# Third feed-forward: the output projection of an attention tile, moved into the next tile's first group

## The reference, cut to what matters

```python
h = shift_token(x)
q, k, v = split(h @ wqkv, 3)                     # 8 heads of 64
q, k = l2norm(q) * qs, l2norm(k) * ksc           # then rotary
sim = (8 q) k^T      # a window of 64 rows sees itself and the 64 before it
attn = softmax(where(mask, -max, sim))
o = attn @ v
x = x + o @ wo                                   # the projection this change moves
h = layernorm(shift_token(x))
a, g = split(h @ w1 + b1, 2)
x = x + (a * gelu(g)) @ w2 + b2
```

## Time and profile before

| what | us |
|---|---|
| median of three runs | 5603.85 |
| lowest and highest of them | 5593.51, 5620.94 |
| the profiled execution's own time | 5583.52 |
| its span, first to last instruction | 5582.2 |
| mean granted TensorE clock over the span, as a share of full | 0.771 |
| TensorE busy, share of the span | 71% |
| VectorE busy | 54% |
| ScalarE busy | 34% |

### The profile page before, as it was taken

How to read it: one execution, slowest core, us unless ns; L and a number is a source line. 1 busy time by engine, 2 the same in 40 slices (tenths; PEclk the granted TensorE clock), 3 DMA queues, 4 the chain that set the end, 5 groups by cost and what they waited for, 6 DMA issues and landing times.

```text
span 5582.2 us, 94810 instructions
## 1 busy us (share of the span) xinstructions
PE 3985.0 (71%) x39676; PEld 3069.5 (55%) x39676; DVE 3004.8 (54%) x8021; ACT 1910.5 (34%) x4228; POOL 819.3 (15%) x600
## 2 busy tenths in 40 slices
PE   5786958467788787863576858667777777776398
PEld 4574847345555555553455647555544555455377
DVE  4455364335555555556266565656666666665333
ACT  2233232123333333320243242325444455552122
POOL 0000000231111111022500000001121111110544
PEclk6555555688999999985766666668888998897699
DMA  9200000240000000001300000000000000000255
GB/s 262 62 2 1 2 1 2 89 133 1 1 1 1 1 1 1 1 22 24 64 1 1 2 1 2 1 2 1 1 1 1 1 1 1 1 1 17 82 163 139
DMA packets 140860, 152.33 MB, mean 27 GB/s; under 512 B 7808, under 2 KB 128002, under 8 KB 139792
## 3 DMA queue, kind: packets, MB, share of 16 engines
q1 hardware_dynamic: 119024, 128.21, 7.9%
q0 software_dynamic: 21408, 18.05, 1.9%
HBM read 87.38 MB, written 59.76 MB: 26 GB/s over the span
## 4 chain that ended last, share of the span: by engine, by line
PE 48%; DVE 31%; ACT 12%; issue 3%; POOL 3%; DMA 2%; SPq 0%; DVEq 0%; POOLq 0%; ACTq 0%
ACT work L3251 4%; PE banks_lane L801 4%; PE banks_lane L422 3%; PE banks_lane L3688 3%; PE banks_lane L1885 2%; DVE work L2038 2%; PE banks_lane L809 2%; PE banks_lane L3137 2%; PE banks_lane L935 2%; PE banks_lane L3172 2%; PE banks_lane L3117 1%; PE banks_lane L3159 1%; POOL room_l_ffn L569 1%; DVE work L2806 1%; DVE weights L3261 1%
## 5 line engine op out<-in xcount | busy, mean ns | idle before, releaser
L422 PE MATMUL banks_lane<-constants,work 128*128 128x128 f32 x968 | 194.5, 346 | 453.0 <-DVE work L408 206.2
L422 PEld LDWEIGHTS banks_lane<-constants,work 128*128 128x128 f32 x968 | 146.3, 178 | 520.1 <-DVE work L408 193.2
L422 PE MATMUL banks_lane<-constants,weights 128*128 128x128 f32 x596 | 125.0, 346 | 350.0 <-DVE weights L408 94.0
L402 POOL TENSOR_TENSOR weights<-weights,constants 128x4 f32<-128x4 f32 x76 | 78.5, 1033 | 1926.4 <-DVE weights L397 1926.4
L422 PEld LDWEIGHTS banks_lane<-constants,weights 128*128 128x128 f32 x596 | 88.5, 178 | 382.6 <-issue 174.9
L3251 ACT ACTIVATE work<-banks_lane,weights 128x192 f32<-128x192 f32 (+1 forms) x512 | 249.3, 506 | 133.4 <-DVE weights L3348 133.4
L402 POOL TENSOR_TENSOR work<-work,constants 128x4 f32<-128x4 f32 x76 | 77.3, 1018 | 1130.6 <-DVE work L397 1130.6
L3355 POOL TENSOR_TENSOR weights<-weights,constants 128x16 f32<-128x16 f32 x64 | 185.4, 2896 | 377.7 <-DVE weights L3263 377.7
L2038 DVE TENSOR_REDUCE work<-banks_lane 128x2 f32<-128x512 f32 x256 | 158.8, 684 | 77.4 <-PE banks_lane L1899 77.4
L3344 DVE TENSOR_REDUCE weights<-banks_lane 128x2 f32<-128x384 f32 (+1 forms) x256 | 122.5, 521 | 142.0 <-PE banks_lane L3159 142.0
L3172 PE MATMUL banks_lane<-constants,work 128*128 128x128 f32 x896 | 135.7, 298 | 80.8 <-DVE work L3336 42.3
(11 more groups left out here) (780 smaller groups left out, 10845.1 us busy)
## 6 DMA issues: line engine op xcount, KB each, us to landing
work<-experts_dram_l_ffn SPq DMA_DIRECT2D x39, 964.0 KB, 4.9
room_l_ffn<-work SPq DMA_DIRECT2D x30, 1188.0 KB, 15.2
work<-experts_dram_l_ffn SPq DMA_DIRECT2D x23, 512.0 KB, 3.7
weights<-weights_dram SPq DMA_DIRECT2D x1, 4833.5 KB, 14.0
work<-room_l_ffn SPq DMA_DIRECT2D x36, 132.0 KB, 4.0
weights<-weights_dram SPq DMA_DIRECT2D x1, 4112.0 KB, 13.1
weights<-bands_dram SPq DMA_DIRECT2D x1, 4096.0 KB, 13.3
weights<-room_l_ffn SPq DMA_DIRECT2D x26, 132.0 KB, 4.2
```

The costliest lines, as they stand in the source:

```text
L402: pool.tensor_tensor(n.rstd, n.rstd, c("neghalf", cols=(0, n.rstd.shape[1])), ALU.pow).then_inc(*u.pool.step(name))
L422: done = pe.transpose(bank[0:rows, t * P:(t + 1) * P], block, c("ident"))
```

## The change

The phase `out` of tiles 0, 1 and 2 is gone. The four matmuls of tile t - 1 are issued in the phase `values` of step (t, 0), ahead of that step's values matmuls, and into `b[3]` instead of `b[2]`. Their wait on ACT's copy of side 1 is the one that the values matmuls had; it now stands ahead of them. DVE's addition for tile t - 1 stands in the same phase behind the division for the next step. `turn_pe` no longer waits for `attended` ahead of side 0; at step (t, 1) it waits for `attended` of tile t - 1 ahead of side 1, which writes `b[3]`. Tile 3 has its `out` at the end, in `b[2]`, as before.

```diff
             yield f"turn{t}_{group}"
+            pe.wait_ge(*u.act.at(f"turned{t}_{group}"))
+            if group == 0 and t > 0:
+                self.out_pe(pe, u, t - 1, b[3])
             self.values_pe(pe, u, t, group, n)
             yield f"values{t}_{group}"
-            if group == 1:
-                pe.wait_ge(*u.act.at(f"oT{t}_1"))
-                for j in range(L2_FFN_PAIRS):
-                    made = pe.matmul(b[2][:, 0:P], m.oT[:, cols_of(j)], self.w(u, f"o{j}"), start=j == 0,
-                                     stop=j == L2_FFN_PAIRS - 1)
-                made.then_inc(*u.pe.step(f"projected{t}"))
-                yield f"out{t}"
+        self.out_pe(pe, u, TILES - 1, b[2])
+        yield "out"
...
+    def out_pe(self, pe, u, t, bank):
+
+        m = self.lanes[u.lane]
+        pe.wait_ge(*u.act.at(f"oT{t}_1"))
+        for j in range(L2_FFN_PAIRS):
+            made = pe.matmul(bank[:, 0:P], m.oT[:, cols_of(j)], self.w(u, f"o{j}"), start=j == 0, stop=j == L2_FFN_PAIRS - 1)
+        made.then_inc(*u.pe.step(f"projected{t}"))
+
...
             pe.wait_ge(*u.act.at(f"oT{pt}_{pg}"))
-            if pg == 1:
-                pe.wait_ge(*u.dve.at(f"attended{pt}"))
         for side in ((0, 1) if t else (1,)):
+            if side and group == 1 and t > 0:
+                pe.wait_ge(*u.dve.at(f"attended{t - 1}"))
...
-        pe.wait_ge(*u.act.at(f"turned{t}_{group}"))
         if t:
             pe.wait_ge(*u.dve.at(f"turned{t}_{group}"))
...
                 self.weights_dve(dve, u, *L2_FFN_STEPS[n + 1], n + 1)
+            if group == 0 and t > 0:
+                dve.wait_ge(*u.pe.at(f"projected{t - 1}"))
+                dve.tensor_tensor(y[:, t - 1, :], y[:, t - 1, :], b[3][:, 0:P], ALU.add).then_inc(*u.dve.step(f"attended{t - 1}"))
             yield f"values{t}_{group}"
-            if group == 1:
-                dve.wait_ge(*u.pe.at(f"projected{t}"))
-                dve.tensor_tensor(y[:, t, :], y[:, t, :], b[2][:, 0:P], ALU.add).then_inc(*u.dve.step(f"attended{t}"))
-                yield f"out{t}"
+        dve.wait_ge(*u.pe.at(f"projected{TILES - 1}"))
+        dve.tensor_tensor(y[:, TILES - 1, :], y[:, TILES - 1, :], b[2][:, 0:P], ALU.add).then_inc(
+            *u.dve.step(f"attended{TILES - 1}"))
+        yield "out"
```

## The result

The changed kernel took 5577.15 us (median of six runs), the kernel before in the same comparison 5608.64 us: a ratio on record of 0.9949, with a 95% interval of 0.9933 to 0.9964 (the two medians alone give 0.9944, 31 us). Two further comparisons of the same two kernels gave 0.9936 (0.9923 to 0.9948) and 0.9919 (0.9903 to 0.9934). The mean of the three, 0.9935, is 36 us of 5600. The prediction said 45 us, a ratio of 0.992. All ratios here use fast executions alone: one of the twelve of the kernel with tile 0's projection moved took 9392 us, at a mean granted clock of 0.42, and is not in its ratio.

A forecast was written before the change was run, and what follows sets the result against it. The out was taken to lie wholly on the chain between tiles in the third feed-forward. Removing it gives 55.75 us, less 10.5 for clock falls: 45.2 us, from 5603.85 to 5559 us; range 5535 to 5580.

The forecast's parts named there:

- The border: At 24 tile boundaries, each window with the out goes, less 0.10 us for the turn's release: 55.75 us gained.
- The cover in first groups: In step (t, 0), TensorE waits of 1.93 us cover 1.89 us of moved work: cost 0, at most 12 us.
- Rival 1: TensorE's cover in first groups is too thin: price 12 us, 33 us left, 5571 us; chance 0.12.
- VectorE's additions and the entry norm: DVE's moved additions cost 0; step (1, 0) with the entry norm counts 0, between -1.7 and +5.9 us.
- The clock: At the 24 changed boundaries, 5.3 falls to the lower clock at 1.98 us each give back 10.5 us.
- My own signs: In the profile, first groups about 8.5 us, wrong above 9; the stage's mean granted clock does not fall.
- The third rival: The clock falls at every changed boundary: 47.5 us against 55.75, 8 us left, 5596 us; chance 0.05.
- The sum and the whole: Over the third feed-forward, 55.75 - 10.5 = 45.2 us gained; the whole median becomes 5559 us, 0.8% less.

## Why the prediction was wrong, point by point

- **The border.** 24 windows at full clock less 0.10 us each are 43.0 us of my 55.75. Measured 42.2 with both kernels filled. Right, and the turn is released as forecast, 1.25 us of waiting included.
- **The cover in first groups: this term failed.** "It fits by 0.05 us", I took 0. Measured 8.60 against 8.46 us, 0.14 in each of the 21 first groups not beside the entry norm, 2.9 us. I had counted 2.035 us for a projection and its values, which take 2.11. Rival 1 in a small form, a quarter of its price.
- **VectorE's additions and the entry norm.** I took 0 for both. The copy moved by 0.1 us under cover. Behind the entry norm steps (1, 1) won 0.7 to 1.7 us each, and steps (1, 0) lost 1.5 and 2.0 us to the low clock in two of the three pairs of the first profile: (1, 0) and (1, 1) together, with the windows of the projections behind (1, 1) taken off, 62.9 us before and 62.3, 64.8 and 62.8 in the three profiles after. Right in sum. Taken apart, at full clock the border behind these steps is worth 10.71 - 9.29 = 1.4 us instead of 1.79, and some 7 us of low clock that these steps (1, 1) had behind waits of 3.05 us are gone.
- **The clock: this step failed.** I counted 12.8 us as a gain, the length of the nine slow projections above full clock, and set 5.3 falls of 1.98 us against it, 10.5 us: in sum, the clock would help by 2.3 us. It hurt by 1.5. The falls themselves came nearly as priced. At or near a changed border the clock fell seven, seven and six times per profile, for 1.9 us each, 12.7 us per profile in the mean. But I spread them over all 24 borders at the rate of 10 in 45, and all but one of them lie behind (0, 1). What had no term at all is tile 0 itself: the low clock of (0, 0) reaches further into (0, 1), 12.4 us instead of 5.5, and (0, 0) takes 1.8 us more, together 8.7 us. It was luck that the sum still came near: the later tiles and the entry norm's steps had lost 19.2 us to the clock before, and only 0.5 of that is left.
- **My own signs.** Two of them came true against me: first groups were to take at most 9 us, and (1, 0) takes 10.17 to 11.55 in four of the five pairs without the entry norm; and the granted clock from the first turn to the last projection fell from 0.89 and 0.90 to 0.88.
- **The third rival** said that the clock falls at every changed border. The Trainium skill ("TensorE: Matmul & The Clock Gate", "Part 4: PE-mode transpose") has the release to full clock not engage for transposes. As I read it there, that a turn right behind waits has the low clock, the rows do not bear it out: in three profiles 47 of 48 turns behind steps (1, 1) and (2, 1) began with their transposes at clock 1.00 right behind 1.25 us of waiting. Whether transposes alone would raise the clock, no run here shows.
- **The sum and the whole.** 37.0 us in the stage instead of 45.2. Of the 8.2 us, 4.4 are missing at full clock (43.0 against 38.6: the cover's 2.9, the entry norm's border 1.1, small pieces the rest) and 3.8 are the clock's (a gain of 2.3 against a loss of 1.5). For the whole, 36 us in the mean of three comparisons, 29 in the first. The median lay in the range, in its upper part.

What stays open is why the low clock reaches further in tile 0 of the changed kernel, and what decides in which pair it ends in step (0, 0), (0, 1) or (1, 0). In the changed kernel pairs 2 to 7 repeat from profile to profile within 0.1 us a step, but pairs 0 and 1 do not: steps (0, 1) and (1, 0) of pair 0 took 8.04 and 10.28 us in the first profile and 10.21 and 12.30 in the second. It changes with a delay elsewhere; I can't compute it from the rows.

## What to carry to other kernels

Take work that nobody waits for off the chain and put it where the engine waits: at full clock the border gave what its windows said, 42.2 us against 43.0, less 2.9 for a cover that was too thin by 0.14 us a step. Count windows at the low clock apart and not as a gain, because the low clock need not leave with the work that stood in it: here the later tiles got rid of 19 us of it, and tile 0 with the step behind it got 20 more. To see what a move is worth without the clock, compare each step with its own length at full clock, or fill TensorE's waits in both kernels with work that nothing reads; the filled pair hides what the moved work costs in its new place. And spread moved work evenly: halves in every step (0.9907, without any useless work) beat the whole in every other (0.9936 in the same comparison), though the intervals all but touch. The shortest attention of all had the changed kernel with its second groups filled by useless matmuls, 553.4 us, at ratios of 0.9894 and 0.9909; as a whole it cannot be told from the halves.

## What was not expected of the hardware

Leaving out work made the stage longer: without 24 projections per lane, attention took 579.7 us against 568.5 to 572.6 with them, while TensorE's waits grew and more steps ran at the lower of its two clocks. Adding 24 useless groups of matmuls per lane made it shorter, 553.4 us. And a memset of 0.485 us per pair cost 24 us over seven gaps, some 3.4 us each: half as a wait of 1.4 to 2.1 us that TensorE did not have before, half as low clock right behind that wait.
